# One core, graph attention with residual layer norm: a loop over eight tiles written out as 64 tiles, and two small bias loads moved forward

## What is computed

```python
def heads(t):
    return t.reshape(b, s, N_HEADS, D_HEAD).transpose(0, 2, 1, 3)
q = heads(x @ Wq + bq)
k = heads(x @ Wk + bk)
v = heads(x @ Wv + bv)
scores = jnp.einsum('bhqd,bhkd->bhqk', q, k) * scale
scores = jnp.where(mask[:, None] == 0, -jnp.inf, scores)
attn = jax.nn.softmax(scores, axis=-1)
out = jnp.einsum('bhqk,bhkd->bhqd', attn, v)
out = out.transpose(0, 2, 1, 3).reshape(b, s, D_MODEL)
return out @ Wo + bo
...
x = _layernorm(x + _L0_gnn_ref(x, adj, ...), axis=-1)
```

## Time and profile before

| | before |
|---|---|
| median of 3 runs | 919.14 us (917.4 to 920.55) |
| the profiled execution, device time | 919.65 us |
| its span in the trace | 917.9 us |
| PE busy | 880.0 us (96%) |
| DVE busy | 797.4 us (87%) |
| POOL busy | 478.7 us (52%) |
| ACT busy | 297.5 us (32%) |
| bytes moved | 58.33 MB, mean 64 GB/s |
| mean granted clock of TensorE | 0.978 of full speed |

### The profile page before, as it was taken

How to read it: one execution, slowest core, us unless ns; L and a number is a source line. 1 busy time by engine, 2 the same in 40 slices (tenths; PEclk the granted TensorE clock), 3 DMA queues, 4 the chain that set the end, 5 groups by cost and what they waited for, 6 DMA issues and landing times.

```text
span 917.9 us, 18281 instructions
## 1 busy us (share of the span) xinstructions
PE 880.0 (96%) x7308; PEld 705.7 (77%) x7308; DVE 797.4 (87%) x1043; ACT 297.5 (32%) x420; POOL 478.7 (52%) x415
## 2 busy tenths in 40 slices
PE   6999999989999899998999989998999999999986
PEld 4777778767787677786877767876777877788865
DVE  3488999969999699997999979998799999999998
ACT  5533333323333233322333323333233233333310
POOL 1165546545556364554565545564455565456652
PEclk9999999989999899999999999999899999999999
DMA  9302113121121212112121120212112111011111
GB/s 332 115 1 76 37 34 99 47 76 47 44 78 47 76 47 76 57 36 88 35 99 47 36 87 36 86 47 74 49 47 86 36 53 43 27 53 47 48 47 46
DMA packets 25564, 58.33 MB, mean 64 GB/s; under 512 B 3088, under 2 KB 5136, under 8 KB 23312
## 3 DMA queue, kind: packets, MB, share of 16 engines
q1 hardware_dynamic: 25488, 57.16, 18.6%
HBM read 40.37 MB, written 16.78 MB: 62 GB/s over the span
## 4 chain that ended last, share of the span: by engine, by line
PE 86%; DVE 7%; issue 4%; SPq 1%; DMA 1%; ACT 0%; POOL 0%; POOLq 0%; DVEq 0%; ACTq 0%
PE psum_v L257 13%; PE psum_v L258 12%; PE psum_v L259 12%; PE psum_s L342 7%; PE psum_ot L357 7%; PE psum_k L258 6%; PE psum_k L259 6%; PE psum_k L257 6%; PE psum_y L376 6%; PE psum_y L380 6%; PE psum_y L377 6%; DVE pt L610 2%; DVE pt L603 2%; DMA adj<-in_adj 1%; DVE soft L585 1%
## 5 line engine op out<-in xcount | busy, mean ns | idle before, releaser
L188 POOL TENSOR_TENSOR soft<-soft,inverse 128x1024 f32<-128x1024 f32 x63 | 128.9, 2047 | 271.3 <-DVE inverse L621 271.3
L742 POOL TENSOR_TENSOR soft<-soft,top 128x1024 f32<-128x1024 f32 x64 | 122.0, 1906 | 126.1 <-DVE top L591 126.1
L610 DVE STREAM_TRANSPOSE pt<-soft 32x512 f32<-32x512 f32 x256 | 180.0, 703 | 4.8
L603 DVE STREAM_TRANSPOSE pt<-soft 64x1024 f32<-64x1024 f32 x128 | 158.0, 1234 | 0.9
L468 ACT ACTIVATE kt<-psum_k,bk_slot,in_slot 128x512 f32<-128x512 f32 x118 | 85.4, 776 | 155.2 <-PE psum_k L259 155.1
L257 PE MATMUL psum_v<-wv_hi,x_hi 128*128 128x512 f32 x256 | 111.0, 433 | 0.0
L451 ACT CAST x_hi<-x_raw 128x512 fp32r<-128x512 f32 x60 | 37.1, 621 | 216.4 <-PE psum_v L259 216.4
L257 PE MATMUL psum_v<-x_hi,wq_hi 128*128 128x512 f32 (+1 forms) x252 | 97.7, 388 | 6.4 <-ACT qt L459 4.3
L258 PE MATMUL psum_v<-wv_lo,x_hi 128*128 128x512 f32 x256 | 103.7, 405 | 0.0
L259 PE MATMUL psum_v<-wv_hi,x_lo 128*128 128x512 f32 x256 | 103.2, 403 | 0.0
L259 PE MATMUL psum_k<-x_hi,wk_lo 128*128 128x512 f32 (+1 forms) x268 | 101.5, 379 | 0.0
(11 more groups left out here) (94 smaller groups left out, 1510.7 us busy)
## 6 DMA issues: line engine op xcount, KB each, us to landing
row<-in_x SPq DMA_DIRECT2D x64, 256.0 KB, 2.9
out_rows<-row SPq DMA_DIRECT2D x64, 256.0 KB, 2.0
x_raw<-in_xt SPq DMA_DIRECT2D x15, 1024.0 KB, 6.0
adj<-in_adj SPq DMA_DIRECT2D x16, 128.0 KB, 2.5
qt<-in_wq SPq DMA_DIRECT2D x4, 256.0 KB, 5.2
x_raw<-in_xt SPq DMA_DIRECT2D x4, 256.0 KB, 5.6
kt<-in_wk SPq DMA_DIRECT2D x4, 256.0 KB, 7.0
row<-in_wv SPq DMA_DIRECT2D x1, 1024.0 KB, 7.7
```

The lines of the kernel that those rows point to most:

```text
L188: ops.tensor_tensor(by_head(soft[:, c % 2, :]), by_head(soft[:, c % 2, :]), inverse[:, c % 2, :].unsqueeze(2).to_broadcast([P, HEADS, NODES]),
L603: last = nc.vector.transpose(pt[own, :, own], by_head(soft[own, c % 2, :]))
L610: last = nc.vector.transpose(pt[k0:k0 + SQ, :, q0:q0 + SQ], by_head(soft[q0:q0 + SQ, c % 2, :])[:, :, keys])
L742: nc.gpsimd.tensor_tensor(by_head(soft[:, c % 2, :]), by_head(soft[:, c % 2, :]), top[:, c % 2, :].unsqueeze(2).to_broadcast([P, HEADS, NO ...
```

## The change

Two things. `run_slots` has no hardware loop any more: all 67 slots are written out on every engine, with constants in place of registers. And the start is reordered: bq and bk are loaded right behind the first pieces of Wq and x with a semaphore of their own, bv and bo keep their place with another; ACT waits for the first pair alone; DVE waits for the second; and POOL makes `bk_slot` before `make_bias(0, 0)`. On POOL the clearing of `pt` moves behind that of two small tiles.

```diff
-        b_in = sem("b_in")
+        qk_b_in, vo_b_in = sem("qk_b_in"), sem("vo_b_in")
...
         def run_slots(eng, slot):
-            for c in range(GT):
-                slot(0, c)
-            with eng.Fori(0, (GROUPS - 1 - PEELED) // 2) as i:
-                for c in range(GT, GT + LOOP):
-                    slot(i, c)
-            for c in range(TILES - PEELED * GT, TILES + 3):
+            for c in range(TILES + 3):
                 slot(0, c)
...
             for kc in range(KC):
                 sp.dma_start(w_raw[0][:, kc, :], w_dram[0][:, kc, :]).then_inc(wq_in[kc], DMA)
                 sp.dma_start(x_raw[:, 0, kc, :], xt_dram[0, :, kc, :]).then_inc(x0_in[kc], DMA)
+                if kc == 0:
+                    for dst, src in zip((bq, bk), b_dram):
+                        sp.dma_start(dst[:, :], src).then_inc(qk_b_in, DMA)
             for kc in range(KC):
                 sp.dma_start(w_raw[1][:, kc, :], w_dram[1][:, kc, :]).then_inc(wk_in[kc], DMA)
-            for dst, src in zip((bq, bk, bv, bo), b_dram):
-                sp.dma_start(dst[:, :], src).then_inc(b_in, DMA)
+            for dst, src in zip((bv, bo), b_dram[2:]):
+                sp.dma_start(dst[:, :], src).then_inc(vo_b_in, DMA)
...
-            act.wait_ge(b_in, DMA * 4)
+            act.wait_ge(qk_b_in, DMA * 2)
...
-            dve.wait_ge(b_in, DMA * 4)
+            dve.wait_ge(vo_b_in, DMA * 2)
...
-            nc.gpsimd.memset(pt[:, :, :], 0.0)
             nc.gpsimd.memset(eps[:, :], EPS)
-            nc.gpsimd.memset(minus_half[:, :], -0.5).then_inc(const_done, 1)
+            nc.gpsimd.memset(minus_half[:, :], -0.5)
+            nc.gpsimd.memset(pt[:, :, :], 0.0).then_inc(const_done, 1)
             pool.wait_ge(const_done, 1)
-            make_bias(0, 0)
-            pool.wait_ge(b_in, DMA * 4)
+            pool.wait_ge(qk_b_in, DMA * 2)
             for s in range(2):
                 nc.gpsimd.tensor_scalar(bk_slot[:, s, :], bk[:, :], in_slot[:, s:s + 1], None,
                                         ALU.mult).then_inc(bk_done, 1)
+            make_bias(0, 0)
+            pool.wait_ge(vo_b_in, DMA * 2)
             run_slots(pool, slot)
```

## The result

The changed kernel takes 884.67 us in the median of four runs (884.1 to 885.31), the kernel before on the same chip 919.85 us (917.4 to 920.96). The ratio is 0.9621 with a 95% interval of 0.9600 to 0.9643. The prediction was 884.4 us. The profiled execution, the longest of the four, took 885.31 us with a span of 883.3 us, 34.6 us less than the span before.

The account below looks back on a forecast made before the run. TensorE, busy 880.0 of 917.9 us, was taken as the bound, losing time to jumps back and a start stall. 28.5 + 6.7 = 35.2 us off 919.65 gave 884.5, kept as 884.4; range 881.5 to 891.5 for 8 in 10.

Parts of the forecast that it names:

- The loop written out: Slots loop: removing five jumps back on TensorE gains 28.5 us, 5.7 each, some 3.4 stall and the rest slower clock.
- TensorE's pace of 13.26 us a slot: First loop pass: eight slots in 106.08 us with PE busy throughout; VectorE has 1.0 us to spare per slot.
- packet counts: Instruction transfers of some 16 KB, 7 in the first pass and 9 in the second, read as PE refetching its body.
- The rule that spoke against it: Skill's instruction-fetch section: limited room, refilled in blocks of 256; written-out slots make all engines stream what the loop kept.
- the first rival: Written-out slots: other engines stall at instruction block borders, about 5 us each, giving 959 us; chance 3%.
- The start: Kernel start: earlier bk spares TensorE a 4.28 us stall and 2.9 us of lower clock; net 6.7 us, 6.0 to 7.2.
- SP's delay: Start, SP's queue: two bias-load issues delay pieces of Wq, x and Wk by 1.2 us at most; taken as 0.5.
- cover: Start: Wv lands at 17.3 us and ACT needs it at 18.6, leaving 1.3 us.
- The sum: Whole kernel: 28.5 + 6.7 = 35.2 us off the profiled 919.65 us, so 884.5; 884.4 kept as prediction.

Follow-up runs that it names:

- short loops: Against the fully written-out kernel: TensorE's weights-times-v product of five tiles done three times, twice in a two-pass hardware loop over 16 matmuls; 893.06 us, 893.79 without that loop.
- the jump a slot later: Against the kernel where TensorE alone keeps the loop: TensorE's passes run over slots 5 to 12 in place of 4 to 11; 906.65 us.

## Why the prediction was right

**The loop written out.** The step was that each jump back costs TensorE's stall and the clock after it, 28.47 us by the difference of the passes. Measured in the trace: 28.5. The medians give 27.6 us with the new start (911.71 less 884.14). That TensorE's pace of 13.26 us a slot holds without pauses was right too. The cost lies with TensorE only (884.14 us with the others looped) and with the jump over a long body (short loops: 893.06 against 893.79 us). That the stall is a fetch of instructions, which the prediction only read out of packet counts (9 in a pass that follows a jump, for 7), is shown by the one packet that each of the 22 long jumps waited for. What the 1.0 us or more ahead of it and the 1.4 us behind it are spent on is open, and so is why the clock lost 1.5 us after some jumps and 2.9 after others.

**The rule that spoke against it** describes something that does happen, but at no cost. By the Trainium skill (Runtime: NRT & Kernel Launch, section Instruction fetch mechanics) each engine's instructions are brought in block by block as it runs, and written-out slots make the other engines' blocks come all along. They do: q14 has 20 packets in place of the 9 of the kernel before. It is hidden fully, since all six stretches took 106.08 us; the first rival, with its 959 us, is out. The same section of the Trainium skill gives TensorE room for 2048 instructions. The kernel before, with five jumps over 1792 matmuls and loads, does not agree that the start of the body was still at hand.

**The start.** The forecast was 7.2 us less 0.5 us for SP's delay, and 6.9 was measured, with 0.3 us of delay in this pair of traces. How much of that is SP's is not shown: with the same start the last matmul of the first quarter of k began anywhere from 16.33 (TensorE alone written out) to 16.81 us (all engines in the loop), and with the loads at their old place from 16.25 to 16.54. Each other step is in the trace. Two details were off without an effect. bk landed by 4.9 us and not 8.6, because I took its landing from a full queue; its two copies then took 1.22 us and not 0.59. And the mask and Wv landed about 1.2 us later than I had them: `make_bias` starts at 19.10 us (before: 17.92), and Wv, which I gave 1.3 us of cover, was split at 18.60, at once after ACT's read of k. By the issue list, its landing took 9.3 us from 9.33 on, so 18.6: the cover was gone, and a little more would have stood in ACT's way. Part of this is the run: with the same start and only TensorE written out, the two came at 18.06 and 18.10.

Of the start's two halves, the prediction did not say which one does it. The order on POOL does, with the semaphore of their own; moving the loads ahead is not needed (884.44 us against 890.74 without POOL's order).

**The sum.** 35.2 us were forecast, and the medians differ by 35.2 (919.85 less 884.67); the spans of the two profiled executions differ by 34.6. The end of the kernel, which the sum held to be unchanged, took 0.9 us more in the profiled one. That the figure of 884.4 is met to 0.3 us is partly luck: the sum started from the profiled execution, 919.65 us, and from the median of the runs known then, 919.14, it would have been 883.9 and not the 884.4 that the prediction kept.

## What to carry to other kernels

Look at the branch itself in the trace: here a hardware loop was free on the four engines with short bodies, and cost a stall of over 3 us, mostly with a slower clock behind it, at each jump of the engine with 896 matmuls in the body. Between that and the 16 matmuls of the short loops nothing was measured. Only that engine has to be written out, or its passes made fewer. When an engine waits behind a chain of small preparations, look first at what stands ahead of them in their own queue: here a wait for the mask held up two copies of 0.59 us together, and the transfers would have been in time where they were.

## What was not expected of the hardware

Where the jump stood mattered more through the clock than through the stall. The profiled execution with TensorE alone in the loop had a span of 912.4 us, and with the jump a slot later 902.1 us. The five stalls, 18.9 and 16.0 us together, make 2.9 of these 10.3 us. The rest is that the clock of TensorE stayed at 1.00 after pauses of 3.07, 3.17 and 3.10 us: PE was busy for 877.2 us and for 869.5. After the 19 other jumps that were profiled, with pauses from 3.18 us on, it fell each time, and the pass took 1.5 to 2.9 us more than stall and work. The shortest of them, in the kernel with the new start and all engines in the loop:

```profile
521.28 3.18 issue
```

That the length of the pause decides is not shown by three pauses on one side, all in one kernel and at another place of the slots. These three are also from the shortest of its four runs, 904.05 us; the longest took 910.71, while the runs of the written-out kernel lie within 1.2 us.
